# A transformer block on one core: the feed-forward half's second product from rounded parts in three terms

## The chip, the cores and the metric

The program runs on one core of one Trainium2 chip. The metric is the device time of one execution in microseconds (us). The engines are PE (TensorE, matrix products), DVE (VectorE), ACT (ScalarE), POOL (GpSimd) and SP (SyncE, which here only issues transfers). Each engine works through its own instructions in order and waits on semaphores for the others.

## The reference, cut to what matters

```python
# x: (2, 2048, 256), float32. First an attention layer with 16 heads of 16 (one pass), then two layers of:
h = shift_token(x)                      # half of the columns moved down by one token
q, k, v = split(h @ wqkv, 3)            # 8 heads of 64
q, k = rotary(l2norm(q)), rotary(l2norm(k))
x = x + local_attention(q, k, v) @ wo   # windows of 128 tokens, keys of this and the last window
h = layernorm(shift_token(x)) * lg + lb
a, g = split(h @ w1 + b1, 2)            # 682 columns each
x = x + (a * gelu(g)) @ w2 + b2         # the second product: contraction over 682
```

Everything is float32 with an output of 2 x 2048 x 256. The second product, `(a * gelu(g)) @ w2`, is the one that is changed.

## The kernel before

The kernel has three blocks one behind the other: `project_phase` (the first attention's products), `attention_phase` (its 32 heads) and `feed_forward_phase` (both further layers). Times below are measured from the start of the span.

In `attention_phase` POOL and SP also prepare weights beside the heads: `prepare_weights` loads a piece of 128x512 numbers, `split_piece` rounds it to the type fp32r (the high part) and subtracts that from the number (the low part), and the parts of wqkv's second layer and of w1 are stored in DRAM. There are 24 such pieces, one per head from head 2 on; the buffers for a piece lie in the space of the cos/sin tables, which are loaded behind them (`load_tables`, at head 27, both tables whole).

`feed_forward_phase` works on 64 tiles of 128 tokens: 32 of each layer, taken in turn from the two batches. It runs in steps t = -1, 0, 1, ...; each engine has its own list of what it does in a step, written out by hand, and the lists meet only through semaphores. A tile v goes through: `transposed_x`, `project` (q, k, v as three terms, high x high, high x low, low x high, of fp32r parts), rotary (ACT copies and squares the product, DVE makes `cosines` and `square_norms`, POOL `sines` and `inverse_norms`, DVE `rotate` and `scale_keys`), `transposed_q_k`, `scores`, DVE's `mask_and_maximum`, ACT's `exponentials`, `normalise` on POOL and DVE, `transposed_probs`, `outputs_of_heads`, `attended`; then DVE's `mean_and_variance`, `transposed_hidden_in`, POOL's `split_y`, and for each pair of tiles `hidden` (the product with w1, three terms of fp32r parts), ACT's `gelu`, DVE's `gated`, and for each tile of the pair `hidden_out`, the second product. Its result is added by DVE's `add_hidden`.

An even step holds `hidden` in two halves of three chunks (lines 1289). An odd step holds `hidden_out` twice (line 1358): for the first tile of the pair ahead of `project`, for the second behind `transposed_hidden_in`. PE's order in an odd step is: `scores` (L1222), `hidden_out`, `project` (L1191), `transposed_probs` (L1261), `transposed_hidden_in` (L1237), `hidden_out`, `outputs_of_heads` (L1303), `transposed_q_k` (L1326), `attended` (L1342), `transposed_x` (L1175). ACT's order: `exponentials` (L1429), `copy_projected` (L1440, L1441, L1443), `copy_PT` (L1450), `affine` (L1458), `gelu` in even steps (L1470), `copy_oT` (L1478), `copy_qT_kT` (L1483, L1485), `round_xT` (L1490, L1492). DVE's: `mask_and_maximum` (L1586) with `split_xT` (L1605), `add_hidden` (L1617), `mean_and_variance`, `normalise` (L1600), `cosines` (L1643), `normalise_mid`, `copy_PT` (L1657), `square_norms` (L1651), `rotate`, `gated` in even steps (L1678), `scale_keys` (L1671), `add_attended` (L1684). POOL's: `normalise` (L1046), `inverse_deviation`, `add_b2`, `sines` (L1067), `inverse_norms` (L1074, L1076), `split_y` (L1084, L1086), and `rotary_tables` for every second tile (L1039).

`hidden_out` takes plain float32 operands: six chunks of the contraction, the last over 64 rows. Each such product stands as two instructions in the trace, so a tile has 12 of them. The operand `act_T` is the space of `gate`, in which `gated` multiplies in place.

wqkv's second layer is loaded in two transfers: the high part at the start of the block into a place of its own (in `k_stack`), the low part by ACT in step 29 over the first layer's.

Of the kernel before, what the change touches and what calls it, by code (L numbers as in the profile page):

```python
# [6 lines left out]
F32 = mybir.dt.float32  # L7
BF16 = mybir.dt.bfloat16
F32R = mybir.dt.float32r
# [4 lines left out]
P = 128  # L14
# [369 lines left out]
def attention_phase(nc, ins, division, VO, mask_sb, weights, ident, load_output_weights, stacks, qkT_stored):  # L384

    with ExitStack() as ctx:
# [3 lines left out]
        q_stack, k_stack, q_minus_first = stacks.q, stacks.k, stacks.q_minus  # L390
        v_ones = sb("v_ones", [P, BODY, TB, VW])
        probs = sb("probs", [P, PROBS, 512])
        excess = probs[:, PROBS - BLOCKS:].rearrange("p (i k) c -> p i k c", i=2)
        spare_pieces = weights.tables[:].rearrange("p a t h d -> p (a t h d)").rearrange("p (i c) -> p i c", c=PIECE)
        raw_piece, piece_hi, piece_lo = spare_pieces[:, 0], spare_pieces[:, 1].bitcast(F32R), spare_pieces[:, 2].bitcast(F32R)
# [61 lines left out]
        def _(sp):  # L457
# [33 lines left out]
            for n in range(NH):  # L491
# [16 lines left out]
                if n == TABLES_HEAD:  # L508
                    sp.wait_ge(weights.parts_stored, 32 * (len(PIECES) - IN_PLACE))
                    weights.load_tables(sp, ins)  # L510
# [9 lines left out]
        def _(pool):  # L520
# [23 lines left out]
            def split_piece(i):  # L544
# [3 lines left out]
                if i < IN_PLACE:  # L548
                    _, _, k, columns = PIECES[i]
                    hi, lo = weights.wqkv_hi[0][:, k, columns], weights.wqkv_lo[:, k, columns]  # L550
# [154 lines left out]
        def _(dve):  # L705
# [52 lines left out]

LAYERS = 2
# [16 lines left out]
          + [("w1", l, k, slice(a, min(a + PIECE, W1_COLUMNS))) for l in range(LAYERS) for k in range(NC) for a in range(0, W1_COLUMNS, PIECE)])  # L776
# [3 lines left out]
class Weights:  # L780


    def __init__(self, nc, ctx, stacks):
# [5 lines left out]
        self.wqkv_hi = [sb("wqkv2_hi0", [P, NC, 3 * INNER], F32R)]  # L789
        self.wqkv_lo = sb("wqkv2_lo", [P, NC, 3 * INNER], F32R)  # L790
        self.tables = sb("tables2", [P, 2, TB, 2, D2 // 2])
# [8 lines left out]
        self.tables_loaded, self.small_loaded = sem("tables2_loaded"), sem("small2_loaded")  # L800
        self.wqkv1_loaded, self.w1_loaded, self.wo_loaded, self.w2_loaded = (sem(n) for n in ("wqkv2_1_loaded", "w1_2_loaded", "wo2_loaded", "w2_loaded"))

    def place_wide(self, ctx, stacks):
# [5 lines left out]
        self.w2 = sb("w2_sb", [P, HC, C])  # L809

    def place_second(self, in_k):

        self.wqkv_hi.append(in_k(NC, 3 * INNER))

    def raw_piece(self, ins, i):
        name, l, k, columns = PIECES[i]
        return ins[name][l].rearrange("(k p) n -> p k n", p=P)[:, k, columns]

    def stored_piece(self, i, part):
        name, l, k, columns = PIECES[i]  # L820
        return self.wqkv_parts[part, :, k, columns] if name == "wqkv2" else self.w1_parts[l, part, :, k, columns]

    def load_tables(self, eng, ins):
        for i, name in enumerate(("cos2", "sin2")):
            eng.dma_start(self.tables[:, i], ins[name].rearrange("(t p) (a d) -> p t a d", p=P, a=2)).then_inc(self.tables_loaded, 16)
# [18 lines left out]
    def load_w2(self, eng, ins, l):  # L844
# [1061 lines left out]
```

## Time and profile before

| | |
|---|---|
| median of 3 runs | 2899.4 us (2896.85 to 2901.22) |
| the profiled execution | 2897.1 us, of it the span 2895.3 us |
| mean granted TensorE clock | 0.981 of full |
| PE busy | 2801.9 us (97%) |
| DVE busy | 2321.7 us (80%) |
| ACT busy | 2114.5 us (73%) |
| POOL busy | 959.5 us (33%) |
| `feed_forward_phase` | from about 1503 us to the end |

The shares are means over blocks with different limits. In the timeline, a row gives start and duration in us, the engine, the line, what is written and read, the count, and in brackets how long the engine had stood idle and who ended that. The granted clock is given as a share of 2.4 GHz; a row of 0.50 is its other level, 1.2 GHz.

### The profile page before, as it was taken

The numbers are of one execution on the slowest core, as the hardware profiler recorded it, in microseconds if no ns is written. First come the engines' busy times: TensorE is split into PE (matmuls) and PEld (weight loads), VectorE is DVE, ScalarE is ACT, GpSimd is POOL, SyncE is SP. The second block draws the span as 40 slices with busy tenths as digits, with TensorE's granted clock in tenths as the row PEclk, the third lists the DMA queues.
The fourth block names the chain that finished last, engine by engine and source line by source line (L and its number), as shares of the span: only waits on it lengthen the run. The fifth ranks groups of instructions, "written<-read, shape, count | busy, mean of one in ns | idle before, by whom it ended". The sixth has DMA issues, their size and how long they took to land. (4 is left out here: it accounts for less than half of the span.)

```text
span 2895.3 us, 59150 instructions
## 1 busy us (share of the span) xinstructions
PE 2801.9 (97%) x22608; PEld 1752.8 (61%) x22608; DVE 2321.7 (80%) x4287; ACT 2114.5 (73%) x4556; POOL 959.5 (33%) x1102
## 2 busy tenths in 40 slices
PE   7999999999999999999997899999999999999997
PEld 7743333333333333333346788888888888888886
DVE  7779999999999999999817677777776777777774
ACT  5568888888888888888866566667666676666764
POOL 7600000010001000000016555555554555655563
PEclk9869999999999999999999899999999999999999
DMA  5703324443444244324203000000000100000000
GB/s 165 190 18 53 53 44 60 62 71 57 73 61 69 53 74 60 69 40 73 41 20 132 11 5 4 5 4 5 5 4 34 55 12 19 19 19 11 20 18 25
DMA packets 85944, 131.33 MB, mean 45 GB/s; under 512 B 33120, under 2 KB 59168, under 8 KB 78240
## 3 DMA queue, kind: packets, MB, share of 16 engines
q1 hardware_dynamic: 79376, 120.41, 21.3%
q10 hardware_dynamic: 6288, 7.14, 0.8%
q8 instruction: 181, 2.97, 0.5%
q14 instruction: 99, 0.81, 0.1%
HBM read 83.98 MB, written 34.61 MB: 41 GB/s over the span
## 5 line engine op out<-in xcount | busy, mean ns | idle before, releaser
L684 ACT ACTIVATE probs<-scores 128x512 f32<-128x512 f32 x2048 | 1115.5, 596 | 199.8 <-PE scores L610 76.4
L717 DVE TENSOR_REDUCE mx<-aux 128x1 f32<-128x1024 f32 x982 | 1201.1, 1223 | 62.8 <-PE aux L578 55.5
L578 PE MATMUL aux<-k_stack,q_stack 48*128 48x512 f32 x2006 | 756.8, 453 | 7.8 <-DMA k_stack<-qk_dram 5.8
L610 PE MATMUL scores<-q_stack,k_stack 50*128 50x512 f32 x2048 | 762.6, 450 | 0.0
L623 PE MATMUL pv<-probs,v_ones 128*32 128x256 f32 x8192 | 657.7, 393 | 0.1
L610 PEld LDWEIGHTS scores<-q_stack,k_stack 50*128 50x128 f32 x2048 | 309.9, 185 | 428.1 <-ACT probs L684 410.5
L623 PEld LDWEIGHTS pv<-probs,v_ones 128*32 128x32 f32 x8192 | 161.6, 108 | 361.0 <-ACT probs L684 290.9
L578 PEld LDWEIGHTS aux<-k_stack,q_stack 48*128 48x128 f32 x2006 | 306.1, 188 | 40.8 <-DVE mx L717 19.5
L531 POOL CAST m_parts<-head_max 128x16 fp32r<-128x16 f32 x32 | 6.3, 198 | 941.4 <-DVE head_max L710 941.4
L1429 ACT ACTIVATE VO<-VO,tables_small 128x256 f32<-128x256 f32 (+1 forms) x512 | 250.9, 491 | 48.5 <-DVE tables_small L1586 48.2
L1289 PE MATMUL bank<-q_minus_first,q_stack 128*128 128x256 f32 x2112 | 270.1, 286 | 2.2 <-POOL q_minus_first L1086 2.2
L1289 PEld LDWEIGHTS bank<-q_minus_first,q_stack 128*128 128x128 f32 x2112 | 258.0, 192 | 12.6 <-issue 9.9
L1586 DVE CUSTOM_DVE_ANT_0 VO<-bank,mask_sb,tables_small 128x256 f32<-128x256 f32 (+1 forms) x512 | 216.1, 469 | 52.0 <-PE bank L1222 52.0
L1046 POOL TENSOR_TENSOR VO<-VO,tables_small 128x512 f32<-128x512 f32 (+1 forms) x128 | 127.3, 1015 | 349.5 <-DVE tables_small L1594 349.5
L1067 POOL TENSOR_TENSOR VO<-VO,tables_small 128x512 f32<-128x512 f32 x128 | 165.3, 1312 | 103.1 <-issue 103.1
L1358 PE MATMUL bank<-w_sb,gate 128*128 128x256 f32 (+1 forms) x768 | 192.7, 393 | 1.1 <-DVE gate L1678 1.1
L1076 POOL TENSOR_TENSOR tables_small<-tables_small 128x16 f32<-128x16 f32 x64 | 189.6, 2962 | 5.3
L1358 PEld LDWEIGHTS bank<-w_sb,gate 128*128 128x128 f32 (+1 forms) x768 | 135.2, 189 | 46.4 <-issue 31.7
L1191 PE MATMUL bank<-wqkv_lo,k_stack 128*128 128x512 f32 x384 | 152.2, 396 | 0.0
L1478 ACT COPY oT<-bank 128x512 f32<-128x512 f32 x64 | 37.6, 587 | 154.0 <-PE bank L1303 154.0
L1440 ACT COPY VO<-bank 128x512 f32<-128x512 f32 x128 | 75.1, 587 | 83.9 <-PE bank L1191 83.9
L1191 PE MATMUL bank<-wqkv_hi,k_stack 128*128 128x512 f32 x384 | 128.6, 403 | 6.7 <-DVE tables_small L1586 4.2
(173 smaller groups left out, 4328.8 us busy)
## 6 DMA issues: line engine op xcount, KB each, us to landing
q_stack<-qk_dram SPq DMA_DIRECT2D x192, 128.0 KB, 5.3
k_stack<-qk_dram SPq DMA_DIRECT2D x192, 128.0 KB, 7.2
qk_dram<-qkT_hi SPq DMA_DIRECT2D x32, 256.0 KB, 3.8
qk_dram<-qkT_lo SPq DMA_DIRECT2D x32, 256.0 KB, 3.9
VO<-o_stage SPq DMA_DIRECT2D x128, 32.0 KB, 7.0
q_minus_first<-sums_dram SPq DMA_DIRECT2D x32, 128.0 KB, 2.9
w_parts<-tables SPq DMA_DIRECT2D x16, 256.0 KB, 2.5
x_dram<-x_sb SPq DMA_DIRECT2D x16, 256.0 KB, 2.0
```

What stands on the lines that cost most here:

```text
L578: return nc.tensor.matmul(out, q_stack[max_rows, n % BODY, tile * P:(tile + 1) * P], k_stack[max_rows, n % BODY, keys * 512:(keys + 1) * 512],
L610: last = nc.tensor.matmul(out, k_stack[0:SCORE_ROWS, n % BODY, s * P:(s + 1) * P], q_stack[0:SCORE_ROWS, n % BODY, j * 512:(j + 1) * 512], ...
L623: last = nc.tensor.matmul(pv[VW * j:VW * (j + 1), columns], v_ones[:, n % BODY, s, :], probs[:, (BLOCKS * step + j) % PROBS, columns], sta ...
L684: nc.scalar.activation(probs[:, e % PROBS], scores[:, item_of_exp(e) % BANKS1], ACT.Exp, scale=float(D1) ** -0.5).then_inc(act_emptied, 1)
L717: nc.vector.tensor_reduce(mx[:, n % BODY, tile, half:half + 1], aux[:, unit % 2].rearrange("p a k -> p (a k)"), AX.X, ALU.max).then_inc(dv ...
L1067: last = nc.gpsimd.tensor_tensor(out=o4[:, :, :, lo:lo + D2 // 2], in0=q4[:, :, :, hi:hi + D2 // 2], in1=sin_table[:, v // 2 % 2, :, lo:lo ...
L1076: nc.gpsimd.tensor_tensor(out=rnorm[:, v % 2], in0=norm2_min, in1=minus_half, op=ALU.pow).then_inc(rnorm_made, 1)
L1191: last = nc.tensor.matmul(bank[QKV_BANK[a]][:], x_part[:, v % 4, k, tokens], w_part[:, k, columns], start=(k == 0 and n == 0), stop=(k == ...
L1289: last = nc.tensor.matmul(out_half, w_part[:, k, chunk * P:(chunk + 1) * P], h_part[:, p % 2, k], start=(k == 0 and n == 0), stop=(k == NC ...
L1358: last = nc.tensor.matmul(bank[F_BANK[v % 2]][:, 0:C], act_T[rows, c, v % 2 * P:(v % 2 + 1) * P], w2_sb[rows, c], start=(c == 0), stop=(c ...
L1429: last = nc.scalar.activation(probs[j][:, u, keys], probs[j][:, u, keys], ACT.Exp, scale=-1.0, bias=negmax[:, j, u:u + 1], accum_out=sums[ ...
L1586: last = nc.vector.tensor_tensor_reduce(out=probs[j][:, u, at:at + n_keys], in0=src[:, 2 * u * P + at:2 * u * P + at + n_keys], in1=mask_s ...
```

## The change

- `hidden_out` computes the second product as three terms of fp32r parts (high x high, high x low, low x high): 18 products of 128 rows for a tile. The low terms come three chunks behind the high ones (`LOW_BEHIND`).
- `gated` writes into `gate`; a new `round_hidden` on ACT copies `gate` to `act_hi` (two copies of 128x768 for a pair, one ahead of `round_xT` of the even step and one behind it), and a new `split_hidden` on POOL makes `act_lo` (two subtractions of 128x768, behind `split_y` of the even step). The last chunk's lower 64 rows of `gate` are set to zero once, and it is contracted over 128 rows.
- w2 is prepared in parts like w1: 6 more pieces in the heads' stretch (30 in all), with buffers of their own, and each layer's w2 is two transfers of 768 KB instead of one.
- The cos/sin tables are loaded by pairs of tiles, two transfers in every odd step, ahead of need by one pair.
- Both parts of wqkv's second layer are loaded by ACT in step 29, since `act_hi` and `act_lo` take the place that the high part had.

```diff
+LOW_BEHIND = 3
...
-          + [("w1", l, k, slice(a, min(a + PIECE, W1_COLUMNS))) for l in range(LAYERS) for k in range(NC) for a in range(0, W1_COLUMNS, PIECE)])
+          + [("w1", l, k, slice(a, min(a + PIECE, W1_COLUMNS))) for l in range(LAYERS) for k in range(NC) for a in range(0, W1_COLUMNS, PIECE)]
+          + [("w2", l, None, slice(a, a + PIECE)) for l in range(LAYERS) for a in range(0, HC * C, PIECE)])
...
-    def load_second_wqkv(self, eng, part):
-        place = (self.wqkv_hi[1], self.wqkv_lo)[part]
-        eng.dma_start(place[:].bitcast(F32), self.wqkv_parts[part]).then_inc(self.wqkv1_loaded, 16)
+    def load_second_wqkv(self, eng):
+        for part, place in enumerate((self.wqkv_hi, self.wqkv_lo)):
+            eng.dma_start(place[:].bitcast(F32), self.wqkv_parts[part]).then_inc(self.wqkv1_loaded, 16)
...
-            weights.load_second_wqkv(sp, 0)
             for t in steps:
+                if t % 2 == 1 and exists(t + 5):
+                    p = (t + 5) // 2
+                    sp.wait_ge(tables_made, 2 * (p - 1))
+                    weights.load_tables(sp, ins, p)
...
+            nc.gpsimd.memset(gate[HR:P, HW], 0.0).then_inc(columns_made, 1)
...
+            def split_hidden(p):
+
+                for i in range(2):
+                    chunks = slice(i * HC // 2, (i + 1) * HC // 2)
+                    pool.wait_ge(act_high_made, 2 * p + i + 1)
+                    nc.gpsimd.tensor_tensor(out=act_lo[:, chunks], in0=gate[:, chunks], in1=act_hi[:, chunks], op=ALU.subtract).then_inc(act_split, 1)
...
                 if exists(t):
                     split_y(t)
+                if t % 2 == 0 and exists(t - 2):
+                    split_hidden((t - 2) // 2)
...
-                pe.wait_ge(act_made, HC * (v // 2 + 1))
...
-                for c in range(HC):
-                    rows = slice(0, P if c < HW else HR)
-                    last = nc.tensor.matmul(bank[F_BANK[v % 2]][:, 0:C], act_T[rows, c, v % 2 * P:(v % 2 + 1) * P], w2_sb[rows, c], start=(c == 0), stop=(c == HC - 1))
+                out, tokens = bank[F_BANK[v % 2]][:, 0:C], slice(v % 2 * P, (v % 2 + 1) * P)
+
+                def high_terms(c):
+
+                    if c % (HC // 2) == 0:
+                        pe.wait_ge(act_high_made, 2 * (v // 2) + c // (HC // 2) + 1)
+                    nc.tensor.matmul(out, act_hi[:, c, tokens], w2_hi[:, c], start=(c == 0), stop=False)
+                    nc.tensor.matmul(out, act_hi[:, c, tokens], w2_lo[:, c], start=False, stop=False)
+
+                def low_term(c):
+
+                    if c % (HC // 2) == 0:
+                        pe.wait_ge(act_split, 2 * (v // 2) + c // (HC // 2) + 1)
+                    return nc.tensor.matmul(out, act_lo[:, c, tokens], w2_hi[:, c], start=False, stop=(c == HC - 1))
+
+                for c in range(HC + LOW_BEHIND):
+                    if c < HC:
+                        high_terms(c)
+                    if c >= LOW_BEHIND:
+                        last = low_term(c - LOW_BEHIND)
...
-                        act.wait_ge(F_done, 2 * p)
+                        act.wait_ge(act_split, 2 * p)
...
+            def round_hidden(p, i):
+
+                chunks = slice(i * HC // 2, (i + 1) * HC // 2)
+                act.wait_ge(act_made, HC * p + chunks.stop)
+                if i == 0 and p:
+                    act.wait_ge(F_done, 2 * p)
+                nc.scalar.copy(act_hi[:, chunks], gate[:, chunks]).then_inc(act_high_made, 1)
...
+                if t % 2 == 0 and exists(t - 2):
+                    round_hidden((t - 2) // 2, 0)
                 if t >= 0 and exists(t + 3):
                     round_xT(t + 3)
+                if t % 2 == 0 and exists(t - 2):
+                    round_hidden((t - 2) // 2, 1)
```

## Rows read from the trace of the kernel before

**Rows 1.** Windows: length; busy of PE, PEld, DVE, ACT, POOL; granted clock; transfers.

```profile
1640.00:2840.00 1200.00, 1186.15 (x8694) 1014.49 (x8693) 881.71 (x2554) 801.67 (x2043) 679.15 (x692) 1.00 0.05 15
```

**Rows 2.** Waits of PE, 1640 to 2840 us: total, times, longest.

```profile
PE bank L1326 <- DVE VO L1671: 13.9, 31, 1.6
```

**Rows 3.** The page's groups of instructions: busy, mean ns, idle before.

```profile
L531 POOL CAST m_parts<-head_max 128x16 fp32r<-128x16 f32 x32 | 6.3, 198 | 941.4 <-DVE head_max L710 941.4
...
L1289 PE MATMUL bank<-q_minus_first,q_stack 128*128 128x256 f32 x2112 | 270.1, 286 | 2.2 <-POOL q_minus_first L1086 2.2
...
L1358 PE MATMUL bank<-w_sb,gate 128*128 128x256 f32 (+1 forms) x768 | 192.7, 393 | 1.1 <-DVE gate L1678 1.1
```

**Rows 4.** Timeline of PE in one odd step.

```profile
2096.26 3.05 PE L1358 MATMUL bank<-w_sb,gate 128*128 128x256 f32 x12
2099.24 0.50 PE L1191 MATMUL bank<-wqkv_hi,k_stack 128*128 128x512 f32 x1
...
2105.49 2.97 PE L1358 MATMUL bank<-w_sb,gate 128*128 128x256 f32 x12
2108.39 1.97 PE L1303 MATMUL bank<-PT,VO 128*64 128x128 f32 x32
2110.75 1.09 PE L1326 MATMUL bank<-ident,VO 128*128 128x128 f32 x8 [0.39 <-DVE VO L1671]
...
2113.40 0.38 PE L1175 MATMUL bank<-ident,x_sb 128*128 128x128 f32 x2
```

**Rows 5.** Timeline of ACT, end of the even step and that odd step.

```profile
2094.44 0.37 ACT L1490 CAST k_stack<-bank 128x256 fp32r<-128x256 f32 x1 [1.31 <-PE bank L1175]
...
2094.89 1.28 ACT L1429 ACT_TABLE_LOAD   x1
2096.43 0.51 ACT L1429 ACTIVATE VO<-VO,tables_small 128x256 f32<-128x256 f32 x1 [0.26 <-DVE tables_small L1586]
...
2100.95 0.59 ACT L1440 COPY VO<-bank 128x512 f32<-128x512 f32 x1 [0.42 <-PE bank L1191]
2101.43 0.61 ACT L1441 ACTIVATE VO<-bank 128x512 f32<-128x512 f32 x1
```

**Rows 6.** Timeline of DVE in that odd step.

```profile
2102.48 0.68 DVE L1643 TENSOR_TENSOR VO<-bank,tables_small 128x512 f32<-128x512 f32 x1
2103.46 0.69 DVE L1643 TENSOR_TENSOR VO<-bank,tables_small 128x512 f32<-128x512 f32 x1 [0.30 <-ACT VO L1441]
...
2109.89 0.80 DVE L1671 TENSOR_TENSOR VO<-VO,tables_small 128x512 f32<-128x512 f32 x1 [1.67 <-POOL tables_small L1076]
```

**Rows 7.** Timeline of POOL: the odd step's first operation.

```profile
2098.57 2.04 POOL L1046 TENSOR_TENSOR VO<-VO,tables_small 128x512 f32<-128x512 f32 x2 [7.00 <-DVE tables_small L1594]
```

**Rows 8.** Timeline of POOL, 1510 us: an addition in SBUF.

```profile
1522.85 1.27 POOL L1115 TENSOR_TENSOR x_sb<-gate,x_sb 128x512 f32<-128x512 f32 x1 [1.08 <-ACT gate L1503]
```

**Rows 9.** Timeline of PE in step 31, the first tiles of layer two.

```profile
2228.32 1.09 PE L1303 MATMUL bank<-PT,VO 128*64 128x128 f32 x16
2231.04 1.97 PE L1326 MATMUL bank<-ident,VO 128*128 128x128 f32 x8 [1.62 <-DVE VO L1671]
...
2235.35 0.38 PE L1175 MATMUL bank<-ident,x_sb 128*128 128x128 f32 x2
```

**Rows 10.** Windows of PE right behind that wait: busy, granted clock.

```profile
2231.00:2234.00 3.00, 2.96 (x11) 0.50 0.01 3
```

**Rows 11.** Timeline of PE, opening of the block: a wait of like length.

```profile
1554.00 1.09 PE L1326 MATMUL bank<-ident,VO 128*128 128x128 f32 x8 [1.22 <-DVE VO L1671]
```

**Rows 12.** Timeline of ACT and PE: the load in step 29 and its first reader.

```profile
2184.57 0.35 ACTq L855 DMA_DIRECT2D wqkv_lo<-wqkv_parts  x1
...
2200.88 0.39 PE L1191 MATMUL bank<-k_stack 128*128 128x512 f32 x1
```

**Rows 13.** Transfers: that load's size and us from issue to landing.

```profile
wqkv_lo<-wqkv_parts ACTq DMA_DIRECT2D x1, 1536.0 KB, 6.6
```

**Rows 14.** Timeline of PE, the last pair's second products.

```profile
2880.06 6.03 PE L1358 MATMUL bank<-w_sb,gate 128*128 128x256 f32 x24 [1.07 <-DVE gate L1678]
```

More of the change, by code:

```diff
@@ L390, in attention_phase @@
         q_stack, k_stack, q_minus_first = stacks.q, stacks.k, stacks.q_minus
+        pieces = sb("weight_pieces", [P, 3, PIECE])
         v_ones = sb("v_ones", [P, BODY, TB, VW])
@@ L393, in attention_phase @@
         excess = probs[:, PROBS - BLOCKS:].rearrange("p (i k) c -> p i k c", i=2)
-        spare_pieces = weights.tables[:].rearrange("p a t h d -> p (a t h d)").rearrange("p (i c) -> p i c", c=PIECE)
-        raw_piece, piece_hi, piece_lo = spare_pieces[:, 0], spare_pieces[:, 1].bitcast(F32R), spare_pieces[:, 2].bitcast(F32R)
+        raw_piece, piece_hi, piece_lo = pieces[:, 0], pieces[:, 1].bitcast(F32R), pieces[:, 2].bitcast(F32R)
         mx = sb("mx", [P, BODY, TB, 2])
@@ L508, in _ @@
                 if n == TABLES_HEAD:
-                    sp.wait_ge(weights.parts_stored, 32 * (len(PIECES) - IN_PLACE))
-                    weights.load_tables(sp, ins)
+                    for p in range(2):
+                        weights.load_tables(sp, ins, p)
                 if n == TABLES_HEAD + 1:
@@ L549, in split_piece @@
                     _, _, k, columns = PIECES[i]
-                    hi, lo = weights.wqkv_hi[0][:, k, columns], weights.wqkv_lo[:, k, columns]
+                    hi, lo = weights.wqkv_hi[:, k, columns], weights.wqkv_lo[:, k, columns]
                 else:
@@ L799, in __init__ @@
         self.b2_dram, self.b2_copied = nc.dram_tensor("b2_copy", (LAYERS, C), F32).ap(), sem("b2_copied")
-        self.tables_loaded, self.small_loaded = sem("tables2_loaded"), sem("small2_loaded")
+        self.tables_loaded, self.small_loaded = [sem(f"tables2_loaded{i}") for i in range(2)], sem("small2_loaded")
         self.wqkv1_loaded, self.w1_loaded, self.wo_loaded, self.w2_loaded = (sem(n) for n in ("wqkv2_1_loaded", "w1_2_loaded", "wo2_loaded", "w2_loaded"))
@@ L842, in load_w1, with load_w2 @@
             eng.dma_start(self.w1[part].bitcast(F32), self.w1_parts[l, part]).then_inc(self.w1_loaded, 16)
-    def load_w2(self, eng, ins, l):
-        eng.dma_start(self.w2[:], ins["w2"][l].rearrange("(k p) n -> p k n", p=P)).then_inc(self.w2_loaded, 16)
+    def load_w2(self, eng, l):
+        for part in range(2):
+            eng.dma_start(self.w2[part][:].rearrange("p k n -> p (k n)").bitcast(F32), self.w2_parts[l, part]).then_inc(self.w2_loaded, 16)
     def load_first(self, eng, ins):
@@ L909, in feed_forward_phase @@
         gate = sb("gate3", [P, HC, 2 * P])
-        act_T = gate
+        act_hi, act_lo = in_k(HC, 2 * P), in_k(HC, 2 * P)
         y_normed = gate[:, 0:4].rearrange("p (s i) c -> p s i c", s=2)
@@ L1038, in rotary_tables @@
                 for table, source, scales in ((cos_table, cos_sb, qks_sb), (sin_table, sin_sb, qks_swapped)):
-                    nc.gpsimd.tensor_tensor(out=by_half(table[:, p % 2]), in0=source[:, position(2 * p)].unsqueeze(2).to_broadcast([P, 2, 2, D2 // 2]),
+                    nc.gpsimd.tensor_tensor(out=by_half(table[:, p % 2]), in0=source[:, p % 2].unsqueeze(2).to_broadcast([P, 2, 2, D2 // 2]),
                                             in1=by_half(scales[:, layer(2 * p)]), op=ALU.mult).then_inc(tables_made, 1)
@@ L1677, in gated @@
                 rows, column = (slice(0, P), j) if j < HW else (slice(0, HR), 2 * HW)
-                nc.vector.scalar_tensor_tensor(act_T[rows, j], bank[H_BANK[j]][rows, 0:2 * P], b1_dve[rows, layer(2 * p), column:column + 1],
+                nc.vector.scalar_tensor_tensor(gate[rows, j], bank[H_BANK[j]][rows, 0:2 * P], b1_dve[rows, layer(2 * p), column:column + 1],
                                                gate[rows, j], ALU.add, ALU.mult).then_inc(act_made, 1)
```

45 lines of the change are left out of this document (24 added, 21 removed).

## The prediction

> **What bounds the kernel now.** I read the windows first, to see which block the changed product lies in and what is full there. From 1640 to 2840 us, 59 or so steps of the feed-forward block with all stages running, PE is busy 1186 of 1200 us at full granted clock; DVE and ACT have 73% and 67% [rows 1]. So PE bounds it, and a shorter product seems to be worth its whole difference. Then I read the waits of PE in the same stretch: there is one kind, 31 times, 13.9 us together, always `transposed_q_k` waiting for DVE's `scale_keys` [rows 2]. The timeline of one pair of steps shows where: in the odd step only, 0.39 us in the one shown, (13.9 - 1.6) / 30 = 0.41 us in the mean of all but the longest [rows 2, 4]. The odd step is the one that holds both `hidden_out`. So there PE is not the bound any more: a chain ends last, and PE's margin over it is already below nothing. The even step has no such wait.
>
> The chain, with the times of the odd step: `scores`, DVE's maxima, ACT's eight exponentials from 2096.43, ACT's copy and square of each half of the projection (2100.95, 2101.43, and the same for the second half), DVE's `cosines` (2102.48 and 2103.46), the norms, POOL's power, `scale_keys` at 2109.89, PE at 2110.75 [rows 4 to 6]. From the second `cosines` to PE it is 7.29 us, whatever PE does meanwhile.
>
> **The products.** A `hidden_out` has 12 instructions of 192.7/768 = 0.251 us, 3.01 us. `hidden`'s products of fp32r parts with 256 moving columns are the nearest row: 270.1/2112 = 0.128 us; 18 of them are 2.30 us [rows 3]. PE saves 0.71 us per tile, 1.42 us per odd step, 45 us over 64 tiles. The last chunk over 128 rows I price like the others, since both means go over all chunks.
>
> **What the chain lets through.** The first `hidden_out` ends 0.7 us earlier, so `project` starts and ends 0.7 us earlier. But ACT gets two copies of 128x768 at the end of the even step. ACT's rows are 0.37 us for 256 columns and 0.59 for 512 [rows 5], so 0.80 for 768 by the same slope. The first copy fits into the 1.31 us for which ACT waits for `transposed_x`. The second lies between `round_xT` and the exponentials' table load: the load starts at 2095.7 instead of 2094.89, the exponentials at 2096.96 instead of 2096.43 (0.26 of the 0.80 goes into the wait that stood there). They end 0.53 us later, at 2101.06; ACT then has no wait left, and the copies and squares follow each 0.48 us apart: the second square ends at 2103.1 instead of 2103.43. DVE is busy without a gap until its first `cosines` ends at 2103.16 [rows 6], so it could not start the second before 2103.1 either. The second `cosines` therefore comes about 0.3 us earlier, and everything behind it too. The rest of the saved 1.42 us becomes waiting of PE: the second `hidden_out` lies behind `project`, where the chain runs beside it. PE's idle time ahead of `transposed_q_k` goes from 0.39 to about 1.5 us (part of it may be taken where `hidden_out` waits for its bank). Bounds: nothing, if ACT's copy takes 1.1 us, to 0.37 us, DVE's limit. 30 such steps by 0.3 us: -9 us.
>
> **The new waits.** POOL gets two subtractions of 128x768. Its addition of 128x512 in SBUF takes 1.27 us [rows 8]; at most in proportion, 1.9 us each. The first can start when the first copy ends (2094.44 - 1.31 + 0.80 = 2093.9 [rows 5]), so they end at 2095.8 and 2097.7. PE wants the second half of `act_lo` for the 16th product of the first `hidden_out`, 2096.26 + 15 x 0.128 = 2098.2; POOL itself is wanted next at 2098.57, and has stood idle for 7.00 us before that [rows 4, 7]. Hidden, with 0.5 and 0.8 us to spare; behind POOL would be queued `normalise`, for which `transposed_probs` waits. `gelu` of the next pair waits for `act_split` from 30 us before: nothing.
>
> **The clock.** PE in the odd step would stand still for about 1.3 to 1.5 us in one piece, behind `outputs_of_heads` and ahead of transposes. The trace has one such place at this point of a step: step 31, where PE waited 1.62 us behind the same group. There the granted clock fell to half [rows 10]: eight transposes took 1.97 us instead of 1.09, and from their start to `transposed_x` it was 2235.35 - 2231.04 = 4.31 us, against 2113.40 - 2110.75 = 2.65 us in the ordinary step [rows 4, 9]: 1.66 us lost. Against that, a wait of 1.22 us in the opening was followed by transposes of 1.09 us [rows 11], at full clock, and the 30 waits of about 0.39 us never cost anything. The new wait is between 1.22 and 1.62 us. So the two ends are no fall in any odd step, 0 us, and a fall in each, 30 x 1.66 = 50 us. Whether one comes depends, by these rows, on how the idle time lies, and the steps drift against it; I take half, 25 us. This loss is not hidden: in the even step PE has no wait to give back.
>
> The Trainium skill (TensorE: Matmul & The Clock Gate, "Why this matters for your kernels") advises against idle gaps between bursts only when they are longer than any that stands here. By that rule the clock would stay up and the sum would lack the 25 us; rows 9 and 10 show a fall behind 1.62 us, and the measurement decides.
>
> **The rest.** Six more pieces are prepared in heads 24 to 29, on a POOL that waits 941 us over the heads [rows 3]: nothing, at most 1 us. One more small fill and a wait for the tables at the block's start: 0.5 us at most. The tables' transfers by pairs are issued by SP behind a shift it has already sent, a pair ahead: nothing. Step 29: the load was issued at 2184.57 and takes 6.6 us; two take 13.2, to 2197.8; the first reader stands at 2200.88 [rows 12, 13]. Hidden by 3 us; if both share the engines with SP's small shifts, up to 3 us once. Last pair: from its first product the old way takes 6.03 us [rows 14]. The new one waits for two roundings and two subtractions of which 0.8 + 1.9 + 1.9 us are exposed before the last three low terms (0.4) and the second tile (2.3): 7.3 us less the 0.6 by which ACT is free before PE started, +0.7; step 63, where both `hidden_out` lie on the path, gives 0.7 back or more. Together 0.
>
> **Sum.** -9 + 25 + 0.5 = +16.5 us. The profiled execution had 2897.1 us (span 2895.3), so 2913.6; the median of the runs lies 2.3 us above it, so about 2916 us, 0.6% slower.
>
> **Rivals.**
> - *The clock stays up.* For it: the wait of 1.22 us without a fall [rows 11], and the skill's rule above. Then -9 + 0.5: 2891 us, with 2887 to 2896 by the chain's bounds. Decides: if the new wait leaves the clock at full in more than about 24 of 30 steps. Chance 0.29; two thirds of it are faster by over 0.2%, the rest within it.
> - *The clock falls in every odd step,* or stays low past one fall: +50 - 9, 2940 us. For it: PE's odd step gets the same wait at the same place each time. Against: the wait is somewhat shorter than 1.62. Chance 0.08.
> - *POOL is late.* If a subtraction takes over 2.2 us, the low terms' second half is late and the first `hidden_out` stretches; at 3 us each PE would wait some 1.5 us per odd step and `normalise` too: +40 us, 2940. The row of 1.27 speaks against. Chance 0.06.
> - *The whole 45 us come through:* 2854 us. It needs the chain to shrink with PE; nothing does that, since the wait of 0.39 us stands in the odd steps already. Chance 0.05.
> - Forecast, 2902 to 2925 us: 0.52.
>
> A measurement of this kernel tells about 0.2% (6 us) from no change. Faster: 0.19 + 0.05 = 0.24. Within: 0.10 of the clock rival and 0.06 of the forecast's lower end, 0.16. Slower: 0.60. The range 2889 to 2928 leaves out the last rivals and the ends of the others. It spans both signs; the forecast's own range is 2902 to 2925.
>
> **What would show it.** In the changed profile: `hidden_out` at 18 x 0.128 us; the exponentials of odd steps starting 0.5 us later after the scores; PE's wait for `scale_keys` in odd steps grown to over 1 us (30 to 45 us in all instead of 13.9); transposes of 1.97 us and granted clock 0.50 behind some of these waits, and a mean clock of the stretch of 0.97 or so instead of 1.00. Wrong if these transposes stay at 1.09 us, if the wait does not grow, or if PE waits inside `hidden_out`.

## The result and the profile after

The changed kernel takes 2881.7 us (median of 7 runs, 2874.7 to 2891.0) against 2899.4 us for the kernel before on the same chip (7 runs, 2893.0 to 2918.5): ratio 0.9933, 95% interval 0.9904 to 0.9962. It is faster by 0.7%, where 2916 us, 0.6% slower, was forecast; 2881.7 lies below the range of 2889 to 2928, and below the 2887 to 2896 of the rival in which the clock stays up. The profiled execution took 2884.1 us, its span 2882.3.

The windows of the steady block first. Columns as in [rows 1]; the second row, in columns of PE alone, is the place behind the longest wait of the stretch, which answers to [rows 10].

```profile
1640.00:2820.00 1180.00, 1141.84 (x9021) 1014.56 (x9020) 875.64 (x2548) 839.11 (x2103) 784.03 (x749) 1.00 0.06 18
2227.00:2230.00 3.00, 2.85 (x18) 1.00 0.01 3
```

PE has 38 us of idle time now where it had 14, and the granted clock is 1.00 all the same: the larger of the forecast's two terms is simply absent. The waits of PE, as in [rows 2], say where the idle time stands:

```profile
PE bank L1342 <- DVE VO L1715: 34.5, 30, 2.3
```

It is the same wait for `scale_keys`, in the odd steps alone, grown from a mean of 0.41 us to 1.11 us. The timeline of PE in one odd step (its `scores` start at 2051.87; in [rows 4] they started at 2094.34), with the first product of each term and the group behind:

```profile
2053.80 0.39 PE L1377 MATMUL bank<-w_hi,k_stack 128*128 128x256 f32 x1
...
2056.03 0.39 PE L1207 MATMUL bank<-wqkv_hi,k_stack 128*128 128x512 f32 x1
...
2062.18 0.38 PE L1377 MATMUL bank<-w_hi,k_stack 128*128 128x256 f32 x1
...
2064.50 1.97 PE L1319 MATMUL bank<-PT,VO 128*64 128x128 f32 x32
2067.57 1.09 PE L1342 MATMUL bank<-ident,VO 128*128 128x128 f32 x8 [1.11 <-DVE VO L1715]
...
2070.23 0.38 PE L1191 MATMUL bank<-ident,x_sb 128*128 128x128 f32 x2
```

From its start to the next product, `hidden_out` takes 2056.03 - 2053.80 = 2.23 us and 2064.50 - 2062.18 = 2.32 us, where [rows 4] have 2.98 and 2.90: 1.33 us less in an odd step. (The trace's names are those of buffers: `w_hi` and `k_stack` hold the parts of w2 and of the activations.) ACT, DVE and POOL in the same step, the rows that answer to [rows 5 to 7]:

```profile
2050.70 0.83 ACT L1513 CAST k_stack<-gate 128x768 fp32r<-128x768 f32 x1
...
2052.30 0.84 ACT L1513 CAST k_stack<-gate 128x768 fp32r<-128x768 f32 x1
2053.16 1.28 ACT L1461 ACT_TABLE_LOAD   x1
2054.46 0.51 ACT L1461 ACTIVATE VO<-VO,tables_small 128x256 f32<-128x256 f32 x1
...
2059.84 0.60 ACT L1473 ACTIVATE VO<-bank 128x512 f32<-128x512 f32 x1
```

```profile
2059.93 1.28 DVE L1687 TENSOR_TENSOR VO<-bank,tables_small 128x512 f32<-128x512 f32 x2
2061.12 0.40 DVE L1680 TENSOR_SCALAR wo_bo_sb<-x_mid,tables_small 128x256 f32<-128x256 f32 x1
2061.45 0.68 DVE L1701 COPY PT<-bank 128x512 f32<-128x512 f32 x1
2062.05 1.20 DVE L1695 TENSOR_REDUCE tables_small<-VO 128x16 f32<-128x1024 f32 x1
...
2066.72 0.80 DVE L1715 TENSOR_TENSOR VO<-VO,tables_small 128x512 f32<-128x512 f32 x1 [1.67 <-POOL tables_small L1083]
```

```profile
2051.60 3.65 POOL L1100 TENSOR_TENSOR k_stack<-gate,k_stack 128x768 fp32r<-128x768 f32 x2 [2.50 <-ACT k_stack L1513]
2056.11 2.04 POOL L1053 TENSOR_TENSOR VO<-VO,tables_small 128x512 f32<-128x512 f32 x2 [0.85 <-DVE tables_small L1638]
```

The exponentials start 2.59 us after `scores` (before: 2.09), as forecast, and POOL's two subtractions end 0.86 us before it is wanted. But `scale_keys` starts at 14.85 us after `scores` instead of 15.55. That makes the odd step 18.67 us instead of 19.39, from one `scores` to the next; the even one is 21.03 in both. All 63 steps together take 1261.7 us instead of 1281.3, 19.6 us less. Against it stand 0.8 us more behind the last `scores` and 5.8 us ahead of the first; the profiled execution is 13.0 us shorter.

### The profile page after: what moved, and what is told of

The parts are those of the page before. It is cut to its first block and busy times, and to the rows that moved or that the text cites. A ratio compares the mean times of both kernels' runs of the same rounds, so it can differ in the third digit from the quotient of the medians.

```text
span 2882.3 us, 60204 instructions
## 1 busy us (share of the span) xinstructions
PE 2756.7 (96%) x22992; PEld 1750.5 (61%) x22992; DVE 2315.0 (80%) x4287; ACT 2151.2 (75%) x4620; POOL 1086.3 (38%) x1179
## 5 line engine op out<-in xcount | busy, mean ns | idle before, releaser
L1207 PE MATMUL bank<-wqkv_hi,k_stack 128*128 128x512 f32 x768 | 251.7, 395 | 5.2 <-DVE tables_small L1630 2.6
L1207 PEld LDWEIGHTS bank<-wqkv_hi,k_stack 128*128 128x128 f32 x768 | 144.3, 188 | 37.3 <-DVE k_stack L1654 3.1
L1100 POOL TENSOR_TENSOR k_stack<-gate,k_stack 128x768 fp32r<-128x768 f32 x64 | 116.8, 1846 | 87.0 <-ACT k_stack L1513 87.0
L1319 PE MATMUL bank<-PT,VO 128*64 128x128 f32 x1984 | 125.7, 280 | 5.0 <-issue 3.1
```

Source lines behind the costliest of these rows:

```text
L1207: last = nc.tensor.matmul(bank[QKV_BANK[a]][:], x_part[:, v % 4, k, tokens], w_part[:, k, columns], start=(k == 0 and n == 0), stop=(k == ...
L1319: last = nc.tensor.matmul(bank[OT_BANK][half * D2:(half + 1) * D2, c * P:(c + 1) * P], v_sb[:, v % 2 + 2 * kb, (2 * c + half) * D2:(2 * c ...
```

## The experiments

Times are medians, with the time of the kernel before on the same chip; a "step" is the time from one `scores` to the next in the profiled execution.

**The changed kernel again, keys first, and the old products** ran together. Keys first means that POOL's power over both halves becomes two, the keys' half first, so that `scale_keys` needn't wait for the other:

```diff
-nc.gpsimd.tensor_tensor(out=rnorm[:, v % 2], in0=norm2_min, in1=minus_half, op=ALU.pow).then_inc(rnorm_made, 1)
+nc.gpsimd.tensor_tensor(out=rnorm[:, v % 2, H2:], in0=norm2_min[:, H2:], in1=minus_half[:, H2:], op=ALU.pow).then_inc(rnorm_made, 1)
+nc.gpsimd.tensor_tensor(out=rnorm[:, v % 2, 0:H2], in0=norm2_min[:, 0:H2], in1=minus_half[:, 0:H2], op=ALU.pow).then_inc(rnorm_q_made, 1)
...
+                if j == 0:
+                    dve.wait_ge(rnorm_q_made, v + 1)
```

In the old products everything of the change stays but `hidden_out`:

```diff
+                pe.wait_ge(act_made, HC * (v // 2 + 1))
+                for c in range(HC):
+                    rows = slice(0, P if c < HW else HR)
+                    last = nc.tensor.matmul(bank[F_BANK[v % 2]][:, 0:C], gate[rows, c, v % 2 * P:(v % 2 + 1) * P], w2_hi[rows, c].bitcast(F32), start=(c == 0), stop=(c == HC - 1))
```

> The changed kernel as it is, for the same chip as the next three. Measure in all of these: the length of an ordinary odd step, from its first scores product to that of the next step (19.38 to 19.41 us before, 18.67 us in the changed kernel's first profile; even steps 21.02 us in both). Chain theory (in odd steps a chain over ACT, DVE and POOL sets when the q and k transposes start, PE waits 1.1 us there): 18.67 us again, ratio about 0.993. Clock theory of the prediction (that wait makes the granted clock fall in half of the odd steps): steps of 20.3 us among them; the first profile showed none.

> The changed kernel, but POOL's power for the inverse norms is split: first the 8 columns of the keys, which scale_keys waits for, then the 8 of the queries, which are wanted only a step later. From POOL's powers of 1, 2, 4 and 16 columns (0.55, 0.73, 1.01, 2.94 us) 8 columns take about 1.65 us, so the chain gets 1.3 us shorter. Chain theory: PE's wait of 1.1 us in odd steps goes, an odd step takes about 17.6 us, 30 x 1.1 = 33 us less in all, ratio to before about 0.982. Rival (the wait only moves to the next thing that is late, DVE or ACT): odd step over 18.3 us, less than 12 us gained.

> The kernel before with the same split of POOL's power. Chain theory: its wait in odd steps was only 0.39 us, so 30 x 0.39 = 12 us less, odd step 19.0 us, ratio 0.996; the difference between this and the changed kernel with the split is then nearly the whole of what PE saves in the products, 1.42 us per odd step. Rival: the same gain in both, then the chain was not what took the products' gain.

> The changed kernel with the products of before: 12 plain float32 instructions per tile on gate and w2's high part (w2's low part is left out of the result), while ACT's two roundings and POOL's two subtractions per pair stay. It shows what the added work costs alone. Chain theory: the exponentials of odd steps start 0.5 us later, but PE is later still with the projection; odd step 19.4 us as before, ratio 1.000 to 1.001. Rival (the added work lengthens the chain one for one, 0.5 us per odd step): 19.9 us, ratio 1.005.

Before on this chip: 2895.5 us.

- The changed kernel: 2879.6 us, ratio 0.9945 (0.9925 to 0.9965); odd steps 18.67.
- Old products: 2892.6 us, ratio 0.9994 (0.9978 to 1.001); odd steps 19.39, the length of before. The roundings, the subtractions, the further pieces and the tables cost nothing that this can tell; the gain is the products'.
- Keys first on before: 2874.0 us, ratio 0.9928 (0.9906 to 0.9951); odd steps 18.94, PE's waits 0.2 us in all. So the chain did end last before. It gained 21.5 us where 12 were expected: 29 ordinary odd steps by 0.45 us make 13, the two steps at the start of layer two gave 4 more, and the first steps and the opening the rest.
- Keys first on the changed kernel: 2872.6 us, ratio 0.9921 (0.9899 to 0.9942), no more than on before, although its products are shorter by 1.3 us per odd step. One odd step was at 17.60, most others at 18.70 and, from step 37 on, 19.05, where 17.6 was expected: something new stood in the way.

**One `hidden_out` made longer.** Six further products of the same shape stand ahead of the 18, in the `hidden_out` ahead of `project` (v even) or in that behind it (v odd):

```diff
+                if v % 2 == 0:
+                    pe.wait_ge(act_high_made, 2 * (v // 2) + 1)
+                    for _ in range(6):
+                        nc.tensor.matmul(out, act_hi[:, 0, tokens], w2_hi[:, 0], start=True, stop=True)
```

> The changed kernel; the first hidden_out of each odd step (the one ahead of project) gets 6 more products of 0.12 us, whose sum is thrown away by the next start, so that it is about as long as before. Chain theory: what the change gained lies here; odd step 18.67 + 0.7 = 19.4 us, wait ahead of the q and k transposes 0.4 us longer or equal. Rival (products count wherever they stand): 0.72 us in this as in the next.

> The changed kernel; the second hidden_out (behind project) gets the 6 more products instead. Chain theory: they go into PE's wait, which shrinks from 1.1 to 0.4 us; the odd step stays 18.67 us. Rival: 19.4 us.

The first made long, the odd step goes from 18.67 to 19.24 and PE's wait stays at 33.4 us in 30; the second made long, the step stays at 18.67 and the wait falls from 34.5 to 14.2 us, 0.40 us per odd step instead of 1.11. (One execution each, 2897.4 and 2896.5; the second began its `scores` 11 us later than the changed kernel, before any of this.) So it is shown: only the `hidden_out` ahead of `project` is on the path, and what the other saves becomes waiting. The first run shows more, which is used below: its second `cosines` starts 0.32 us later after `scores` than in the changed kernel (8.97 against 8.65), and DVE's reduction follows 1.75 us behind that instead of 1.52.

**ACT's second rounding made short, and POOL made slow.** In the first, `act_hi`'s second half gets 4 columns of 256, so that its products are wrong; in the second, one further power of 2 columns (0.74 us, its result unused) stands ahead of POOL's power in every step:

```diff
-                nc.scalar.copy(act_hi[:, chunks], gate[:, chunks]).then_inc(act_high_made, 1)
+                if i == 0 or p == 0:
+                    nc.scalar.copy(act_hi[:, chunks], gate[:, chunks]).then_inc(act_high_made, 1)
+                else:
+                    nc.scalar.copy(act_hi[:, chunks, 0:4], gate[:, chunks, 0:4]).then_inc(act_high_made, 1)
```

```diff
+                nc.gpsimd.tensor_tensor(out=idle_out, in0=norm2_min[:, 0:2], in1=minus_half[:, 0:2], op=ALU.pow)
```

> The changed kernel, but ACT's second rounding takes 3 x 4 columns instead of 3 x 256 (the last three chunks of act_hi keep old numbers from the first pair on). Step of the prediction under test: that ACT's added 0.5 us sets the chain. If ACT sets it, the odd step gets up to 0.3 us shorter (18.4). If DVE sets it (in the changed kernel's trace the second cosines start right behind the first, without a wait), 18.67 us as it is.

> The changed kernel with one more power of 128x2 on POOL (0.73 us) ahead of the inverse norms, so that PE's wait in odd steps grows from 1.1 to about 1.8 us; even steps get about 0.4 us. Clock theory of the prediction (a wait of over 1.6 us at this place makes the clock fall in half of the steps, 1.66 us each): odd steps of 19.4 and of about 21 us side by side, granted clock 0.50 behind some waits. Rival (the clock stays up behind such waits, and the fall in step 31 of before needed more than its 1.62 us): all odd steps 19.4 us.

Less work for ACT made the kernel slower: odd steps of 19.67 us, 2909.5 us in one execution. The timeline of DVE shows the place, and that of POOL the reason:

```profile
2068.77 1.27 DVE L1690 TENSOR_TENSOR VO<-bank,tables_small 128x512 f32<-128x512 f32 x2
2069.97 1.41 DVE L1683 TENSOR_SCALAR wo_bo_sb<-x_mid,tables_small 128x256 f32<-128x256 f32 x1
```

```profile
2068.59 2.63 POOL L1074 TENSOR_TENSOR VO<-VO,tables_small 128x512 f32<-128x512 f32 x2 [0.29 <-issue]
```

`normalise_mid` takes 0.40 us in the changed kernel and 1.41 here. POOL's sines are two operations; here they start 0.3 us earlier, the second at 2069.95, just ahead of DVE's 2069.97, and DVE's ends 0.16 us behind it. The instruction is as long (1.39 to 1.52 us) in the three odd steps of the changed kernel that lasted 19.9 to 20.0 us, and in keys first on the changed kernel (1.49 us in nearly all of its odd steps, 0.40 in the short one). The Trainium skill (SBUF — State Buffer, "Who interferes with whom") says that VectorE and GpSimd share a pair of SBUF ports, that the one that issues first holds it for its whole instruction, and that the other is blocked. The page counts this form of instruction, `tensor_scalar`, among those that can do so. By that rule the order of the starts decides; this trace agrees (1.41 us with POOL 0.02 us ahead, 0.40 in the changed kernel with DVE 0.19 us ahead), but in keys first DVE's recorded start is ahead too, by 0.07 to 0.09 us, and DVE is the one held up:

```profile
2048.41 1.50 DVE L1684 TENSOR_SCALAR wo_bo_sb<-x_mid,tables_small 128x256 f32<-128x256 f32 x1
```

```profile
2047.25 2.51 POOL L1075 TENSOR_TENSOR VO<-VO,tables_small 128x512 f32<-128x512 f32 x2 [0.51 <-issue]
```

POOL's second operation starts at 2048.50 here. The next two sets test the order.

POOL made slow (2944.0 us in one execution): odd steps of 19.86 us in layer one, 1.2 us more, and six of 21.3 to 21.6, where the clock fell. The windows (PE alone; behind one of the falls, and behind a wait that had none) and the timeline of the fall:

```profile
1753.00:1756.00 3.00, 3.00 (x14) 0.63 0.00 0
1711.00:1714.00 3.00, 2.99 (x20) 1.00 0.01 3
```

```profile
1752.76 1.09 PE L1344 MATMUL bank<-ident,VO 128*128 128x128 f32 x8 [2.30 <-DVE VO L1717]
1753.69 3.52 PE L1360 MATMUL bank<-wo_sb,oT 128*128 128x256 f32 x8
```

Behind a wait of 2.30 us the eight products of `wo` take 3.52 us instead of 1.89, and the step is 1.68 us longer: the price of a fall was right. But the same wait at 1711 had none, nor had step 31 with a wait of 3.00 us, nor any odd step of layer two, with waits of 2.30 and, from step 37 on, 1.77 us.

**DVE's instruction in another form.** The same normalisation as a `scalar_tensor_tensor`:

```diff
-nc.vector.tensor_scalar(hn[:].rearrange("p (a c) -> p a c", a=2), x_mid[:, v % 4, 0:3:2], mv[:, 0:1], rstd, ALU.subtract, ALU.mult)
+nc.vector.scalar_tensor_tensor(hn[:].rearrange("p (a c) -> p a c", a=2), x_mid[:, v % 4, 0:3:2], mv[:, 0:1], rstd.unsqueeze(1).to_broadcast([P, 2, hn.shape[1] // 2]), ALU.subtract, ALU.mult)
```

> Keys first on the changed kernel, and DVE's normalisation of hn written as a scalar_tensor_tensor with the same result instead of the tensor_scalar. Theory (the collision with POOL's second sines operation belongs to this form of DVE instruction: 0.40 us alone, 1.49 when both are on): the instruction goes from 1.49 back to about 0.4 us, the odd steps of layer one from 18.70 to about 17.6 us, where PE has no wait left (the one such step of e2), those of layer two, which hold 0.35 us more of DVE, from 19.05 to about 17.95; PE's wait for the scaled keys goes from 18.6 us to under 5. About 30 x 1.1 = 33 us less than e2: 2840 us. Rival A (any instruction of DVE that reads and writes SBUF is held up by POOL): the new form lasts 1.49 us too and nothing changes, 2872. Rival B (another link of the chain is next): the instruction goes to 0.4 but the steps gain less than 0.5 us, 2860.

> The kernel before with keys first and the same scalar_tensor_tensor. Theory: PE bounds this kernel already once the keys go first (odd steps 18.93 us, waits of 0.2 us in all), so nothing changes: 18.93 us, 2874 us. With e9 this gives what the products are worth when the chain is out of the way: 1.3 us per odd step, 31 of them 35 to 40 us. Rival A: the same, 2874. Rival B: the same; it would make the difference to e9 under 20 us.

> The changed kernel with the same scalar_tensor_tensor alone. Theory: the collision is met only in three odd steps (3, 35 and 37, 19.9 us instead of 18.67); they go to 18.67, all others keep 18.67: 3.6 us less than the changed kernel, 2878. Rival A: the three long steps stay. If the ordinary steps get shorter as well, the chain's 18.67 held some of the collision too.

> e7 (ACT's second rounding copies 4 columns instead of 256, so that the low parts of the second half are wrong) with the same scalar_tensor_tensor. Theory: e7's odd steps of 19.67 us were the collision, which came up because POOL's sines started 0.3 us earlier; without it they are at 18.3 to 18.6 us, at or below those of the changed kernel, since ACT's chain has 0.57 us less in it. Rival A: still 19.67. Rival: ACT's copy set the 18.67 in full: 18.1.

Before: 2895.2 us.

- On the changed kernel with keys first: 2842.9 us, ratio 0.9833 (0.9797 to 0.987); odd steps 17.67 and 18.03, the instruction 0.47 us (in one ordinary step 1.55, and that step took 18.83).
- On before with keys first: 2873.7 us, ratio 0.9922 (0.9896 to 0.9949); odd steps 18.94, as without it.
- On the changed kernel alone: 2881.0 us, ratio 0.9952 (0.9928 to 0.9976); odd steps 18.79 (the form takes 0.51 to 0.53 us in them, 0.12 more). Two of the long ones stayed, 3 and 37, and they are the two that the repeated changed kernel has as well; step 31 took 21.2 us instead of 19.4, because the clock fell there behind a wait of 2.34 us. The expected 3.6 us did not come.
- With the short copy: the instruction lasts 1.54 us, the odd steps 19.82 us, 2913.6 us in one execution. Here too the clock fell in step 31 (a wait of 2.42 us).

The last run refutes my explanation of the first: the new form is held up just as well. On the changed kernel with keys first it escaped for another reason. There the recorded starts are 2039.33 for DVE and 2039.40 for POOL's second operation, and POOL's took 1.54 us instead of 1.3: this time POOL was held up. In keys first with the old form the starts had the same gap, and DVE was held up.

```profile
2039.33 0.47 DVE L1684 SCALAR_TENSOR_TENSOR wo_bo_sb<-x_mid,tables_small 128x256 f32<-128x256 f32 x1
```

```profile
2038.16 2.78 POOL L1075 TENSOR_TENSOR VO<-VO,tables_small 128x512 f32<-128x512 f32 x2 [0.51 <-issue]
```

All profiles together say where the outcome turns. With the old form DVE was held up (1.37 to 1.52 us) in each of some 100 meetings in which POOL's second operation started from 0.04 us ahead to 0.10 us behind by the record; in each of the more than 600 in which it started 0.12 to 0.25 us behind, DVE took 0.39 to 0.44 us, and POOL's operation was longer the closer it came: 1.42 us at 0.12, 1.35 at 0.19. With the new form the turn lies between 0.00 and 0.05 us. So a recorded lead of up to 0.10 us isn't yet one for `tensor_scalar`; what happens within those 0.10 us no trace shows.

**The order fixed.** `tensor_scalar` again, but POOL's second sines operation waits for it; nothing else is changed:

```diff
                 for lo, hi in ((0, D2 // 2), (D2 // 2, 0)):
+                    if lo and v >= 2:
+                        pool.wait_ge(hn_made, v - 1)
```

and, on the changed kernel without keys first, one or two further operations of 0.25 us on POOL ahead of the power, in the odd steps alone, to set PE's wait:

```diff
+                if v % 2 == 1:
+                    for _ in range(2):
+                        nc.gpsimd.tensor_scalar(idle_out[:, _], norm2_min, 1e-24, None, ALU.max)
```

> Keys first on the changed kernel with the normalisation as it was (tensor_scalar), but POOL's second sines operation waits for it (hn_made). Theory (POOL and DVE can't both be on at this place, and the one that starts first holds the other up for its whole length; in e2 they met within 0.07 us): the instruction takes 0.40 us in every odd step, POOL's second operation starts some 0.3 us later and ends before the norms want POOL, and the odd steps are at 17.6 to 17.7 us in layer one and 18.0 in layer two, as in e9: 2841 us, 31 us under e2. Rival (the form of DVE's instruction matters, not the order): still 1.49 us or POOL late by as much, 2870.

> e7 with the same wait. Theory: the order alone made e7's odd steps 19.67 us; they come to 18.6 to 18.7 us as in the changed kernel (DVE's normalisation starts at the same 9.25 us after the scores in both), so that ACT's second rounding costs the chain nothing any more: 2880 us. Rival (POOL's earlier sines do harm in another way, at DVE's copies or the norms): 19.2 us or more.

> The changed kernel with one more operation of 0.25 us on POOL ahead of the power, in the odd steps alone (result unused). PE's wait in the odd step goes from 1.10 to 1.35 us, the step from 18.67 to 18.92 us. Theory of the prediction (no fall behind 1.22 us, some behind 1.62): a few falls of the granted clock at most, each 1.67 us; 7.5 us more than the changed kernel without one. Rival (the wait's length isn't what decides at these lengths, as step 31 of the changed kernel with 2.35 us and no fall could say): no fall at all.

> The same with two such operations: a wait of 1.60 us, steps of 19.17 us. Theory: falls in some of the odd steps, most of them in layer one, 1.67 us each; with 8 falls 15 + 13 = 28 us more than the changed kernel. Rival: no fall, 15 us more.

Before: 2900.0 us.

- Keys first, order fixed: 2843.5 us, ratio 0.9826 (0.9795 to 0.9858); odd steps 17.60 in layer one, 17.95 in layer two.
- Short copy, order fixed: odd steps 18.66 us instead of 19.67 (one execution, 2869.6 us). The order alone had made it slow, and with 0.57 us less of ACT's work in the step it is no faster than the changed kernel: ACT's second rounding costs nothing, since DVE's second `cosines` starts right behind the first (8.66 us after `scores`) in both.

The same two engines in keys first with the order fixed, DVE, then POOL:

```profile
2037.04 0.40 DVE L1686 TENSOR_SCALAR wo_bo_sb<-x_mid,tables_small 128x256 f32<-128x256 f32 x1
```

```profile
2035.88 1.29 POOL L1077 TENSOR_TENSOR VO<-VO,tables_small 128x512 f32<-128x512 f32 x1 [0.51 <-issue]
2037.52 1.28 POOL L1077 TENSOR_TENSOR VO<-VO,tables_small 128x512 f32<-128x512 f32 x1 [0.34 <-DVE wo_bo_sb L1686]
```

POOL stands 0.34 us for DVE and is still 0.46 us early for the norms. Its window of all engines shows PE as the bound again, 1134.7 of 1140 us:

```profile
1640.00:2780.00 1140.00, 1134.73 (x8968) 1007.63 (x8967) 848.00 (x2540) 832.09 (x2088) 797.07 (x804) 1.00 0.06 19
```

The waits came out longer than set, since POOL's power itself took 3.3 to 3.4 us instead of 2.94 in layer one, but they serve the better. (There it starts 0.11 to 0.14 us behind one of DVE's `rotate`; in layer two, with the `rotate` 0.9 us later, it takes 2.94.) With one further operation PE waits 1.74 us in the odd steps of layer one and 1.32 in those of layer two; with two 2.34 and 1.52. (One execution each, 2890.8 and 2911.2 us.) PE alone, from 1640 us with one and from 1680 us with two, and a typical wait of the latter:

```profile
1640.00:2220.00 580.00, 554.43 (x4398) 1.00 0.04 13
```

```profile
1680.00:2840.00 1160.00, 1100.18 (x8704) 1.00 0.06 19
```

```profile
2206.04 1.09 PE L1346 MATMUL bank<-ident,VO 128*128 128x128 f32 x8 [2.34 <-DVE VO L1719]
```

Up to 2840 us there is one fall with one operation (at 2231, behind a wait of 2.95 us at the start of layer two) and one with two (behind the first wait of 2.34, at 1672). 56 waits of 1.3 to 2.35 us had none, nor had the wait of 3.16 us at the start of layer two with two operations.

## Why the prediction was wrong

**The clock: the step that failed.** The forecast put a fall of the granted clock into half of the odd steps, 25 us. There was none. Two things were wrong in it. The wait was 1.11 us and not 1.3 to 1.5, because the chain gave back more than forecast (below). That was not what mattered: the last two runs put waits of 1.32, 1.52, 1.74 and 2.34 us at the very place, and the clock stayed up behind all but one of them. The inference from two rows, no fall behind 1.22 us [rows 11] and a fall behind 1.62 us [rows 10], that a length between them decides, was unsound. Step 31 alone shows it, the very place of [rows 9]: of the profiles with a wait of 1.6 us or more there, four had a fall (behind 1.62, 2.34, 2.42 and 2.95 us) and nine had none (1.65, 1.68, five times 2.35, 3.00 and 3.16 us), the changed kernel among these with 2.35. The price of a fall, 1.66 us, was right (1.68 and 1.66 where there was one: step 31 of before went from 20.08 to 18.42 us with the old products, for want of a fall). What brings one is not settled by these runs. In the run with POOL made slow in every step, six falls came behind waits of 2.30 us with another of 0.79 in each even step; with waits of 2.34 and none in the even steps there was one. That points to the idle time around a wait, but it is one execution of each, and the first of them had no fall behind 3.00 us in step 31. The rival "the clock stays up" was the one that held for the clock, and it deserved more than 0.29; its time, 2887 to 2896 us, was missed as well, by the chain's term. The Trainium skill (TensorE: Matmul & The Clock Gate, "Why this matters for your kernels") advises only against idle gaps longer than these. This case agrees for the 56 waits without a fall, and differs for the falls behind 1.62 to 2.95 us, where the measurement decides.

**The chain: the term that was mis-sized.** "About 0.3 us" per odd step was 0.72, and 27 steps carry it. The parts, by the rows:
- The exponentials started 0.50 us later, as forecast (0.53).
- The second square ended 0.52 us earlier (8.57 us after `scores` against 9.09), where 0.33 was forecast: the step of 0.48 us by which the copies and squares follow each other was right, the start was taken a little too late. DVE's second `cosines` starts right behind the first and not behind ACT, 8.66 against 9.12 us: 0.46. That is more than the forecast's bound of 0.37 for DVE: the first itself starts 0.08 us earlier, since `add_hidden` ahead of it no longer waits for the end of the first `hidden_out`, and the second follows 0.60 us behind it, not at its recorded end.
- The rest, 0.25 us, was not seen at all. The forecast let the chain from the second `cosines` to PE be 7.29 us "whatever PE does meanwhile". But DVE's copy of the transposed probabilities stands in it, behind `normalise_mid` and ahead of the reduction, and it needs the first 8 of PE's 16 transposes. In the kernel before these began behind `project` at

```profile
2103.53 1.91 PE L1261 MATMUL bank<-ident,VO 128*128 128x128 f32 x16
```

and half of their 1.91 us ends at 2104.5, with the copy at 2104.60. In the changed kernel they come earlier with PE, and the copy follows `normalise_mid` at once. So the reduction starts 1.52 us behind the second `cosines` where it was 1.75. The run with the first `hidden_out` made long isolates it: there it is 1.75 again, with 0.11 us of waiting for PE ahead of the copy, and 1.52 where the second is made long.

The sum: 27 steps of -0.72 (-19.4), three steps that met POOL's sines (+1.6), the first two odd steps (-2.5) and the even ones (+0.8) make -19.6 us, where 30 steps of -0.3 made -9. So the profiled executions differ from the forecast by 29.5 us (-13.0 against +16.5): 25 of the clock and 10.6 of the steps, less 6.1 that the ends cost more than forecast.

**Right.** The products (2.23 and 2.32 us against 2.30 forecast; from start to start they save 1.33 us per odd step instead of 1.42); that only the first counts, and that the second's saving is waiting (the two lengthened versions); ACT's 0.84 us and POOL's 1.83 for 128x768 (0.80 and at most 1.9 forecast); that the helpers, the pieces and the tables cost nothing (old products: 0.9994). The last pair and step 63 together cost 0.8 us behind the last `scores`, where the forecast had the 0.7 us of the one paid back by the other. POOL late: no.

**The opening.** The first `scores` stood 5.8 us later in this profile, 0.5 us forecast. 4.2 us of it were lost by the last exponential of the heads (at 1498.1 us against 1493.9), and the runs don't put that to the change: with the other form of DVE's instruction, which comes later, the changed kernel had its first `scores` at 1554.9 us, before at 1559.1, and over all runs they lie between 1553.0 and 1576.0. From that exponential to the first `scores` the profile has 1.7 us more than before, the repeated changed kernel none. What differs in the heads is where a stretch of low clock lies. The first of the heads' exponentials (at 169 us in before) came 5.3 us earlier than before's, and those at 229 us came 6.7 us later. In the windows of PE alone, first of before, then of after:

```profile
128.00:157.00 29.00, 28.99 (x129) 0.51 0.14 50
...
190.00:213.00 23.00, 22.80 (x219) 1.00 0.16 20
```

```profile
157.00:213.00 56.00, 54.27 (x285) 0.51 0.12 22
```

**"The whole 45 us come through"** had 0.05, with the reason that nothing shrinks the chain with PE. The reason was not quite right, as the parts above show, but the whole didn't come through here. With the chain shortened as well, and the order of DVE and POOL fixed, the odd step goes from 18.94 to 17.60 and 17.95, and the kernel from 2873.7 us (0.9922 of before) to 2843.5 (0.9826): about 28 of the 45 us.

## What to carry to other kernels

When a chain over several engines sets a step, don't take a stretch of it as fixed: look in it for each instruction that waits, also behind the one that matters in its engine's order, for the engine that you make faster. One wait with a fall of the clock behind it is no threshold; before it is put into a sum thirty times, count the waits of that length that had none, or make some. And if less work makes a kernel slower, look for the two engines that now start together: a wait that fixed their order was worth 1.0% here (0.9921 to 0.9826 with keys first), and gave, level with the other form of DVE's instruction, the fastest version: 2843.5 us, 1.7% below the kernel before.

## What the runs showed of the hardware

- A DVE instruction from SBUF to SBUF of 0.40 us (0.47 to 0.57 as `scalar_tensor_tensor`) takes 1.37 to 1.55 us if a POOL `tensor_tensor` of 128x512 starts just before it (0.02 us in the rows shown), and ends about when that one does. With DVE 0.19 us ahead it takes 0.40, and POOL's 1.35; with the order fixed by a wait, 0.40 and 1.29.
- By the recorded starts the outcome turns between 0.10 and 0.12 us of DVE's lead for `tensor_scalar`, and between 0.00 and 0.05 us for `scalar_tensor_tensor`. At 0.07 us the first lost (1.49 us) and the second won (0.47 us, and POOL's operation took 1.54 us).
- PE stood for 1.5 to 2.35 us in every other step of a stretch of 1160 us, and once for 3.16 us, and the granted clock was 1.00 throughout. At one place of one step, waits of 1.6 to 3.2 us had a fall behind them in four profiles and none in nine.
